# A graph-attention and feed-forward kernel: two of ten source tiles aggregated from rounded parts, with the low parts made by GpSimd's transfers

## What is computed

```python
def gat_layer(x, W, att_src, att_dst, bias, src, dst, heads, out_ch, concat):
    h = (x @ W.T).reshape(n, heads, out_ch)
    e = leaky_relu(a_src[src] + a_dst[dst], 0.2)      # a = einsum('nhc,hc->nh', h, att)
    ex = exp(e - segment_max(e, dst)[dst])
    alpha = ex / (segment_sum(ex, dst)[dst] + 1e-16)
    return segment_sum(alpha[:, :, None] * h[src], dst) + bias
h = relu(gat_layer(norm(x), W1, ..., heads=8, out_ch=128))
x = x + gat_layer(h, W2, ..., heads=1, out_ch=768)
x = x + ffn(norm(x))
```

## Time and profile before

| | |
|---|---|
| median of three runs | 719.73 us |
| the profiled execution, its own time | 720.14 us |
| its span, first to last instruction | 718.2 us |
| busy share PE, DVE, ACT, POOL | 98%, 73%, 58%, 15% |
| granted TensorE clock | full in all slices |
| chain that ended last | PE 88%, DVE 4%, DMA 3%, ACT 2% |

### The profile page before, as it was taken

The page is one execution under the profiler, slowest core; times in us unless marked ns, Lnnn a source line. Parts: engine busy times, 40 slices in busy tenths (PEclk is TensorE's granted clock), DMA queues, the critical chain, the costliest instruction groups (busy, mean ns, idle before and its releaser), DMA issues.

```text
span 718.2 us, 13084 instructions
## 1 busy us (share of the span) xinstructions
PE 704.5 (98%) x4599; PEld 657.0 (91%) x4599; DVE 523.7 (73%) x874; ACT 415.6 (58%) x813; POOL 107.4 (15%) x95
## 2 busy tenths in 40 slices
PE   8999999999999999999999999999999999999998
PEld 6799999779899999999999999999999899999987
DVE  5899888698889999999999764445568742837241
ACT  4565574388688888888888864454453334422201
POOL 2567130000000000000000000000223331222211
PEclk9999999999999999999999999999999999999999
DMA  8626655659221212303230352201882634325011
GB/s 286 217 79 198 198 168 168 178 162 323 74 73 37 72 37 72 105 8 101 60 151 0 88 130 65 59 4 35 244 280 64 205 104 174 99 62 190 24 31 58
DMA packets 50225, 84.09 MB, mean 117 GB/s; under 512 B 14633, under 2 KB 35951, under 8 KB 49280
## 3 DMA queue, kind: packets, MB, share of 16 engines
q1 hardware_dynamic: 44492, 65.69, 30.8%
q10 hardware_dynamic: 4500, 13.82, 5.9%
q0 software_dynamic: 1184, 3.92, 1.8%
HBM read 68.09 MB, written 15.33 MB: 116 GB/s over the span
## 4 chain that ended last, share of the span: by engine, by line
PE 88%; DVE 4%; DMA 3%; ACT 2%; issue 1%; POOL 0%; ACTq 0%; SPq 0%; DVEq 0%; POOLq 0%
PE bank L1344 22%; PE bank L1483 13%; PE bank L1410 12%; PE bank L1323 11%; PE bank L1221 11%; PE bank L1559 4%; PE bank L1587 4%; DMA w1n_sb<-in_W 3%; PE bank L1138 3%; PE bank L1464 2%; ACT L L876 1%; DVE x2f L2156 1%; PE bank L1140 1%; PE bank L1153 1%; PE bank L1603 1%
## 5 line engine op out<-in xcount | busy, mean ns | idle before, releaser
L1344 PE MATMUL bank<-PT,h1s 125*128 125x250 f32 x800 | 175.6, 374 | 0.0
L1344 PEld LDWEIGHTS bank<-PT,h1s 125*128 125x128 f32 x800 | 148.6, 190 | 16.0
L1945 DVE SCALAR_TENSOR_TENSOR L<-asb,nadh 125x1250 f32<-125x1250 f32 x80 | 118.1, 1518 | 11.0 <-PE bank L1323 10.4
L889 ACT COPY PT<-bank 125x500 f32<-125x500 f32 x200 | 99.8, 596 | 45.2 <-PE bank L1323 45.2
L1954 DVE CUSTOM_DVE_ANT_0 L<-L,LC 125x1250 f32<-125x1250 f32 x80 | 113.5, 1456 | 0.2
L876 ACT ACTIVATE L<-L,nm 125x1250 f32<-125x1250 f32 x80 | 107.8, 1370 | 0.0
L1323 PEld LDWEIGHTS bank<-ident,L 125*125 125x125 f32 x800 | 93.4, 189 | 4.8 <-ACT L L876 1.7
L1323 PE MATMUL bank<-ident,L 125*125 125x125 f32 x800 | 94.8, 273 | 1.3 <-ACT L L876 0.9
L1751 DVE TENSOR_TENSOR hotr<-iota,r 125x1500 f16<-125x1500 f16 x50 | 46.6, 931 | 8.0 <-PE bank L1140 4.5
L1483 PE MATMUL bank<-h_hi,PT_hi 125*125 125x384 f32 x200 | 41.5, 350 | 0.0
L707 POOL MEMSET pick<- 128x90 f32 x1 | 0.2, 169 | 271.4 <-ACT hT L915 271.4
(11 more groups left out here) (260 smaller groups left out, 1227.3 us busy)
## 6 DMA issues: line engine op xcount, KB each, us to landing
asb<-src_logit_rows SPq DMA_DIRECT2D x7, 1250.0 KB, 5.8
atom_w<-in_atom_inT SPq DMA_DIRECT2D x5, 1152.0 KB, 13.3
atom_w<-in_atom_outT SPq DMA_DIRECT2D x5, 1152.0 KB, 9.3
log_count_scratch<-LCw SPq DMA_DIRECT2D x10, 546.9 KB
LC<-log_count_scratch SPq DMA_DIRECT2D x10, 546.9 KB
LCt<-log_count_scratch SPq DMA_DIRECT2D x10, 546.9 KB
h_scratch<-h1st ACTq DMA_DIRECT2D x10, 448.0 KB
rdT<-reciprocal_scratch SPq DMA_DIRECT2D x8, 500.0 KB, 4.6
```

Source lines behind the costliest of these rows:

```text
L889: act.copy(PT[(k - lag) % 2][:, 2 * b:2 * b + 2, :], bank[turned_bank(first, k - lag, b)][0:NP, 0:2 * GW].rearrange("p (s n) -> p s n", s= ...
L1344: mm = pe.matmul(bank[2 + (k - lag) % 2][:, 0:GW], h1s[q][:, s, :], PT[(k - lag) % 2][:, s, :], start=(s == 0), stop=(s == NT - 1))
L1945: dve.scalar_tensor_tensor(L[r][:, :], asb[q][0:NP, 1, :], nadh[q][:, t:t + 1], asb[q][0:NP, 0, :], ALU.add, ALU.max).then_inc(stt_done, 1)
```

## The change

For heads 1 to 7 the source tiles 2 and 3 (bank 1 of `PT`, `PARTED = 1`) are no longer aggregated in full precision. For them there are three rounded passes over two tiles each, six products instead of two full-precision ones. The feature side comes from DRAM (`parts_scratch`), where the first stage puts for tiles 2 and 3 the high part, the remainder and the negated high part: ScalarE casts (`features_higher`), GpSimd subtracts and negates (`part_features`). For the other side ScalarE evacuates bank 1 twice, negated and unrounded into `PT` and rounded into `PT_hi`. GpSimd then makes the negated low part in `PT_lo` for each of 35 groups: it copies `PT`'s two tiles there by one transfer, waits, and adds `PT_hi` by an accumulating transfer (`accum_op=ALU.add`). TensorE waits for it (`lower_step`) ahead of the third pass. Reciprocal rows of all batches go through one buffer `rrow`, so `rows_out_of` waits for the store of the batch before. Some semaphores of the last stage are merged with those of the heads, and pads shift the SBUF layout.

```diff
@@ SP, load_features and the order around it
                 for a, b in ROWS:
                     sp.dma_start(h1s[q][a:b, :, :], ...).then_inc(head_in[q], 16)
+                    sp.dma_start(h1p[q][a:b, :, :, :].bitcast(F32).rearrange("p l s c -> p (l s) c"),
+                                 parts_d[:, :, ds(h * C + -C, C)].rearrange("l (s p) c -> p (l s) c", p=NP)[a:b, :, :]
+                                 ).then_inc(head_in[q], 16)
...
+            sp.wait_ge(parts_stored, 2 * TWO)
             load_features(1, 1)
@@ GpSimd, first stage
+            def part_features(t):
+                p, spread = t % 2, h1st[t % 2][:, C:HC]
+                pool.tensor_tensor(parted[p][:, 1, :], spread, parted[p][:, 0, :].bitcast(F32), ALU.subtract
+                                   ).then_inc(parted_done, 1)
+                pool.tensor_scalar(parted[p][:, 2, :], parted[p][:, 0, :].bitcast(F32), -1.0, None, ALU.mult
+                                   ).then_inc(parted_done, 1)
+                pool.wait_ge(parted_done, 2 * (t - PT0) + 2)
+                for a, b in ROWS:
+                    pool.dma_start(parts_d...[a:b, t - PT0, :, :], parted[p][a:b, :, :]...).then_inc(parts_stored, 16)
             for t in range(1, NT):
                 scale_by_sums(t)
+                if PT0 + 3 <= t < PT1 + 3:
+                    part_features(t - 3)
@@ GpSimd, heads
+            def lower_parts(hh, kk):
+                n, p = 2 * NG * hh + kk, kk % 2
+                done = 32 * (n + -NG)
+                pool.wait_ge(tb_evac, NG * n + PARTED + 1)
+                alone(pool)
+                pool.dma_start(PT_lo[p][:, :, :].bitcast(F32), PT[p][:, PT0:PT1, :]).then_inc(lower_step, 16)
+                pool.wait_ge(lower_step, done + 16)
+                alone(pool)
+                pool.dma_start(PT_lo[p][:, :, :].bitcast(F32), PT_hi[p][:, :, :].bitcast(F32), accum_op=ALU.add
+                               ).then_inc(lower_step, 16)
+                pool.wait_ge(lower_step, done + 32)
+                alone(pool)
@@ ScalarE
+            def features_higher(t):
+                act.wait_ge(h1_out, t + 1)
+                act.copy(parted[t % 2][:, 0, :], h1st[t % 2][:, C:HC])
...
             for i in range(2, NT):
+                if PT1 <= i - 1 < PT1 + 2:
+                    act.wait_ge(parted_done, 2 * (i - 1 - PT1) + 2)
                 features_out(i - 1)
...
+                if PT0 <= i - 1 < PT1:
+                    features_higher(i - 1)
@@ evac
-                    act.copy(PT[(k - lag) % 2][:, 2 * b:2 * b + 2, :],
-                             bank[turned_bank(first, k - lag, b)]...).then_inc(tb_evac, 1)
+                    if b == PARTED and not (first and k - lag < NG):
+                        act.activation(pair, turned, ACT.Copy, scale=-1.0)
+                        act.copy(PT_hi[(k - lag) % 2][:, :, :], turned).then_inc(tb_evac, 1)
+                    else:
+                        act.copy(pair, turned).then_inc(tb_evac, 1)
@@ rows_out_of
+                freed(act, rden_stored, 16 * m)
+                act.copy(rrow[0:t1 - t0, 0:NP], bank[4][0:t1 - t0, 0:NP]).then_inc(rden_rows, 1)
@@ TensorE, aggregate
+                for s in range(NT):
+                    if plain or not PT0 <= s < PT1:
+                        mm = pe.matmul(sums, h1s[q][:, s, :], PT[p][:, s, :], start=(s == 0), stop=(plain and s == NT - 1))
+                if not plain:
+                    for part in range(3):
+                        if part == 2:
+                            pe.wait_ge(lower_step, 32 * n + (32 - 32 * NG))
+                        for s in range(2):
+                            rows = (PT_lo if part == 2 else PT_hi)[p][:, s, :]
+                            mm = pe.matmul(sums, h1p[q][:, part, s, :], rows, start=False, stop=(part == 2 and s == 1))
+                mm.then_inc(agg_done, 1)
```

More of the change, by code:

```diff
@@ L62 @@
 LATE = 6
+BATCHES = 3 * H // 2
+PARTED = 1
+PT0, PT1 = 2 * PARTED, 2 * PARTED + 2
+HL = HC - C
 FIRST = 8 * NP
@@ L167, in gnn_ffn_kernel @@
         w1n_sb = sb("w1n_sb", [C, H, D], F32, w_ctx)
+        w_ctx.close()
+        w_ctx = ExitStack()
+        parted = [sb(f"parted{p}", [NP, 3, HL], F32R, w_ctx) for p in range(2)]
         w_ctx.close()
@@ L285, in gnn_ffn_kernel @@
         h1s = [sb(f"h1s{q}", [NP, NT, C], F32, p3) for q in range(2)]
[L287 to L289 removed]
+        rrow = sb("rrow", [NT, NP + 3], F32, p3)
+        PT_hi = [sb(f"PT_hi{p}", [NP, 2, GW], F32R, p3) for p in range(2)]
+        PT_lo = [sb(f"PT_lo{p}", [NP, 2, GW], F32R, p3) for p in range(2)]
         rdA = [sb(f"rdA{p}", [C, H, NP], F32, p3) for p in range(2)]
[L291 removed]
+        h1p = [sb(f"h1p{q}", [NP, 3, 2, C], F32R, p3) for q in range(2)]
+        pad3 = sb("pad3", [128, 448], F32, p3)
         PT = [sb(f"PT{s}", [NP, NT, GW], F32, p3) for s in range(2)]
+        once = ExitStack()
+        sb("pad_hT", [C, (H - 1) * N], F32, once)
+        wrow2 = sb("wrow2", [2, HC], F32, once)
+        once.close()
         hT = sb("hT", [C, H, N], F32, p3)
@@ L702, in after_x2 @@
                     add_bias(n + 1)
+            def lower_parts(hh, kk):
[10 more added lines that the diff above has]
+                alone(pool)
+            for kk in range(NG, 2 * NG):
+                lower_parts(0, kk)
+            with pool.Fori(1, H // 2) as hh:
+                for kk in range(2 * NG):
+                    lower_parts(hh, kk)
             pool.wait_ge(agg_done, NG * H)
@@ L1326, in turn_bank, with aggregate @@
                 mm.then_inc(tb_full, 1)
-            def aggregate(hh, k, b, first=False, last=False):
+            def aggregate(hh, k, first=False, last=False):
                 lag = 2
@@ L1332, in aggregate @@
                 q, g, n, h = at(hh, k, lag)
-                if b == 0:
-                    pe.wait_ge(tb_evac, NG * n + NG)
-                    if first and k == lag:
-                        pe.wait_ge(head_first, 2 * TWO)
-                    elif g == 0:
-                        pe.wait_ge(head_in[q], TWO * (hh + 1))
-                    if not (first and k - lag < 2):
-                        pe.wait_ge(agg_out, n + -1)
-                if first and k == lag and b == 4:
-                    pe.wait_ge(head_in[q], TWO * (hh + 1))
-                for s in range(2 * b, 2 * b + 2):
-                    mm = pe.matmul(bank[2 + (k - lag) % 2][:, 0:GW], h1s[q][:, s, :], PT[(k - lag) % 2][:, s, :],
-                                   start=(s == 0), stop=(s == NT - 1))
-                if b == 4:
-                    mm.then_inc(agg_done, 1)
+                p = (k - lag) % 2
+                pe.wait_ge(tb_evac, NG * n + NG)
+                if first and k == lag:
+                    pe.wait_ge(head_first, 2 * TWO)
+                elif g == 0:
+                    pe.wait_ge(head_in[q], 2 * TWO * (hh + q) + TWO * (1 - q))
+                if not (first and k - lag < 2):
+                    pe.wait_ge(agg_out, n + -1)
+                sums = bank[2 + p][:, 0:GW]
+                plain = first and k - lag < NG
+                for s in range(NT):
+                    if first and k == lag and s == 8:
+                        pe.wait_ge(head_in[q], TWO * (hh + 1))
+                    if plain or not PT0 <= s < PT1:
[8 more added lines that the diff above has]
+                mm.then_inc(agg_done, 1)
             def turn_reciprocals(hh, k, first=False, last=False):
@@ L1363, in step @@
                 turn_reciprocals(hh, k, **at_end)
-                for b in range(5):
-                    aggregate(hh, k, b, **at_end)
+                aggregate(hh, k, **at_end)
             pe.wait_ge(ln_done, NT)
```

44 lines of the change are left out of this document (22 added, 22 removed).

## The result

The changed kernel takes 828.4 us, the median of four runs (827.08 to 830.21), where the kernel before took 719.81 beside it: a ratio of 1.149, with an interval from 1.146 to 1.152. The forecast was 718.5, with a range up to 765. The profiled execution took 830.21 us, with a span of 828.3 at a mean granted clock of 0.955.

A forecast was written before the change was run, and what follows sets the result against it. TensorE was taken to set the heads' step, with ScalarE next. Terms of -1.5 - 0.2 + 0.3 + 0.2 = -1.2 us took the median from 719.73 to 718.5, range 716.5 to 765.

The forecast's parts named there:

- GpSimd's chain: Heads 1 to 7: copy, accumulating transfer and waits take 6.2 us a pass, under the step of 6.4.
- the rival's rule: Heads: GpSimd's serial transfers set the step, each 0.1 us over costing 3.5 us; 724 to 760, chance 0.23.
- Its margin: Heads: GpSimd's pass of 6.2 us is under the 6.4 us step by 0.2 only.
- Few engines: GpSimd's transfers: five DMA engines give a pass of 9.1, +93 us, 813; chance 0.09 together with slow accumulation.
- The case's other half: GpSimd's accumulating transfer in the heads is slow; shares the chance of 0.09 with few engines.
- TensorE's narrow products: Heads' aggregation: rounded 250-column products take 0.12 us each, step 6.29; rival at 0.423 each, +59, 779, chance 0.08.
- ScalarE's order: Heads: ScalarE binds next, by the exponentials the transposes wait for; a step of 6.38 to 6.42 us.
- the small gain of 0.8 to 2.2 us: Heads 1 to 7: 35 steps go from 6.444 to 6.38 to 6.42 us, gaining 1.5 in the middle.
- VectorE doesn't starve the queue: Heads: GpSimd's descriptors keep going under VectorE's passes; a transfer issued during such passes landed in 2.1 us.
- The first stage: Added casts and GpSimd arithmetic cost 0.3 us, 0 to 4, up to 8 if blocked; rival about 724, chance 0.08.
- a cost that I had put at nothing: Part loads double SP's feature descriptors, nearly a head ahead of their use; counted among the rest that costs nothing.

The follow-up runs named there:

- e2: Changed kernel with the second, accumulating transfer made a plain copy, low part then wrong: 790.97 us, ratio 1.095.
- e8: Kernel of e1 with ScalarE's rounded copy of the second bank moved behind the next step's exponentials: 722.83 us, ratio 1.002.
- e1: Changed kernel without GpSimd's two transfers in the heads; third pass reads the rounded high part instead: 727.04 us, ratio 1.007.
- e10: Changed kernel with the edits of e7 and e8, features in two parts, first parts' load behind w2n_sb's: 743.96 us, ratio 1.032.
- e11: Kernel of e8 (no transfers) with the first odd head's parts load moved behind w2n_sb's: 720.06 us, ratio 0.9985.
- e12: Changed kernel with both transfers cut to the first of two source tiles, 122 KB in place of 244 KB each: 774.94 us, ratio 1.074.
- e6: Kernel of e1 with GpSimd's first-stage subtractions and negations cut to one column of each tile: 727.09 us, ratio 1.009.
- e7: Changed kernel with the low part made by GpSimd's subtraction in place of copy and accumulation, nothing left out: 741.9 us, ratio 1.030.

## Why the prediction was wrong, point by point

- **GpSimd's chain, the step that failed.** It was put at 6.2 us: copy 2.6, accumulation 3.0, three waits 0.3, collisions 0.3. Measured: 2.8, 3.9, about 1.3 and 1.4, in all 9.4. Each term was too small. The copy's error alone would have left the pass at 6.4, still within the step; each of the other three alone would have taken it to 7.1 to 7.3, which by the rival's rule is already +23 to +30 us, and only together do they make the whole. The copy was nearly right; the accumulation lay nearer to its upper bound (4.4) than to the plain copy that I took (e2: +1.1). A wait for a transfer that has just landed costs 0.6 us until the next one is issued, not 0.1. And a collision costs about 3 us, as written, but 15 of 35 copies met one where I had spread 0.3 over each. By the rival's own rule, (9.4 - 6.44) x 35 = +104 us, which gives 823 of the 828.4. The rule was right and stood at 0.23 chance with a pass of at most 7.6.
- **Its margin.** The forecast rested on 0.2 us of room, with one term measured nowhere; the bounds given for the bare pass, 4.7 to 8.2, held the measured 8.0, and at 8.2 the same rule gives +62 and 781. The range stopped at 765, short of my own bound, and the collisions were not added to that end.
- **Few engines.** The rival's number, 813, is near the result, but not its mechanism: a plain copy of 244 KB lands in 2.8 us, not in the 4.4 that five engines would take. The rule for the number of engines stands in the Trainium skill (DMA: Bandwidth & Descriptors, Why a DMA increments its semaphore by 16 and not by 1), not in the section that the prediction gives. It doesn't bind here, for either transfer. While the packets of the copy and of the accumulation of the pass at 347.62 moved, the 16 DMA engines were busy for 0.77 and 0.94 of the time, where five could reach 0.31 (length, busy time of each engine, granted clock, DMA share, GB/s):

```profile
348.75:349.99 1.24, 1.24 (x8) 1.24 (x7) 0.00 (x0) 0.97 (x3) 0.00 (x0) 0.50 0.77 202
352.41:354.60 2.19, 2.19 (x13) 1.97 (x12) 2.19 (x3) 2.19 (x5) 0.00 (x0) 1.00 0.94 114
```

  The case's other half, accumulation being slow, is right: it makes 38 of the 109 us.
- **TensorE's narrow products: right.** After, where nothing waited:

```profile
507.61 3.55 PE L1410 MATMUL bank<-PT,h1s 125*128 125x250 f32 x16
510.81 0.82 PE L1417 MATMUL bank<-PT_hi,h1p 125*128 125x250 f32 x4
511.47 0.40 PE L1417 MATMUL bank<-PT_lo,h1p 125*128 125x250 f32 x2
511.70 1.64 PE L1410 MATMUL bank<-PT,h1s 125*128 125x250 f32 x7
```

  (511.70 - 507.61 - 16 x 0.2116)/6 = 0.117 us each, against 0.12; the step with them is 6.26 in e8, against 6.29.
- **ScalarE's order: right in kind, too small in size.** It does bind next, but at 6.47 us a step (e1), not 6.38 to 6.42. So the small gain of 0.8 to 2.2 us is none: 35 x (6.47 - 6.44) = +1. Of the 0.55 that the loop grew from its 5.92 of the earlier trace rows, 0.47 is the sixth instruction, as taken, and 0.08 the gap between exponentials and the next copy, which I had held fixed.
- **VectorE doesn't starve the queue: right.** Undisturbed copies landed in 2.8 us under VectorE's passes.
- **The first stage, 0.3 with a range to 8: too small.** The start of the heads came 2.8 us late after the change, 1.0 to 6.9 in the other kernels. Most of the 7.0 at the transposes behind the att2 products lies elsewhere, in a cost that I had put at nothing: the parts' load ahead of w2n_sb's. TensorE's timeline of the kernel after:

```profile
186.35 4.46 PE L1445 MATMUL bank<-w2n_sb,att 128*2 128x256 f32 x48 [2.44 <-DMA w2n_sb<-in_W]
190.74 0.48 PE L1386 MATMUL bank<-ident,L 125*125 125x125 f32 x2
```

  They wait 2.44 us for the load and take 4.39 to the next transposes, at a granted clock of 0.61, where before took 2.70 at 1.00 (181.06 to 183.76). With the load moved behind w2n_sb's, e10 and e11 show no such wait. But it varies where the load stays ahead, too: none in e2, 0.38 us in e12, 2.44 here.
- **What remains open:** why the first stage of one kernel differs by several microseconds from one execution to the next, and what in the change moves it later on average. e6 says only that it is not GpSimd's arithmetic alone. Long copies stand beside SyncE's loads of features and beside its broadcasts; how much each costs was not told apart, nor why a transfer of GpSimd's queue waits for them.

## What to carry to other kernels

Two dependent transfers in a loop cost mostly what doesn't depend on their bytes, here 5 of 8 us a pass. So add up that fixed part of both, the 0.6 us behind each landing and the loads that the queue will meet before you count bytes, and put each at its upper bound where the room is a fifth of a microsecond. What counts for a queue in steady state is the pass, not the latency, and each wait between its transfers is part of the pass; taking one wait away gave 64 us. Where an engine gives work to another, ask first whether the freed engine is still the bound: here two products less on TensorE were worth nothing until one copy on ScalarE was moved, and then 5 us of the heads, which the later start took back.

## What the runs showed of the hardware

- An accumulating transfer of 244 KB from SBUF to SBUF lands 3.9 us after its issue, a plain one after 2.8; at 122 KB 3.0 and 2.2. For the plain copy the Trainium skill (DMA: Bandwidth & Descriptors, Anatomy of one DMA) has a fixed 2 us and the bytes at 436 GB/s, an estimate of 2.6; the trace agrees within 0.2.
- A transfer of GpSimd's queue that is issued beside one of SyncE's loads lands some 3 us later (the copies at 336.05 and 347.62 above). Most of the copies that meet one take 6.0 to 8.0 us against 3.4 in the kernel after, issue to next issue, and 4.1 to 5.9 against 2.7 at half the bytes in e12. Where the timing is alike, within 0.1 us of the first of the feature loads, the delay is the same: 2.6 to 3.0 us (241.43, 288.47, 382.88) and 2.7 to 2.9 (233.07, 270.50 in e12).
- GpSimd's subtraction and VectorE's pass over L and LC (two inputs from SBUF) exclude each other for a whole instruction, and VectorE's TENSOR_SCALAR of two columns was held up in the same way in e7. VectorE lost 0.9 to 1.05 us to a subtraction of 500 columns. A RECIPROCAL of ten columns was not held up: in e10 it took its 0.22 us at 319.75, inside the subtraction from 319.62 to 320.86.
- After a wait of TensorE the granted clock fell. Windows of the kernel after, first the wait, then the transposes behind it, then the first products behind the heads (length, busy time of each engine, granted clock, DMA share, GB/s):

```profile
341.80:346.90 5.10, 0.00 (x0) 0.00 (x0) 1.93 (x5) 0.16 (x1) 0.84 (x1) 1.00 0.63 91
347.50:351.10 3.60, 3.60 (x23) 3.60 (x22) 0.00 (x0) 2.20 (x5) 0.66 (x2) 0.61 0.26 69
523.25:528.14 4.89, 4.89 (x18) 4.89 (x17) 0.00 (x0) 2.80 (x9) 1.25 (x3) 0.53 0.66 191
```

  The clock of the second is 0.61, a mean between the levels of 1.2 and 2.4 GHz, and twenty transposes took 3.5 us from start to start in place of 2.2. It cost nothing in the heads, since no pass of GpSimd waited for ScalarE there but the first. Outside them it cost 1.7 us in the att2 products (4.39 for 2.70) and 1.9 behind the heads (4.89 for 3.02).
